# First attention: transposing the attended rows next to the input rows, with one copy for both and the affinity product at the front of the step

## The chip, the core and the metric

The kernel runs on one core of one Trainium2 chip. The metric is device time in microseconds (us) of one execution, as a median of several. A profile is one further execution with the hardware profiler on; its times are counted from the first instruction. The engines are PE (matrix products; its weight loads are listed as PEld), DVE (vector), ACT (scalar), POOL (GpSimd) and SP (which issues DMAs). Each works through its own queue in order, and they wait for each other at semaphores.

## What is computed

Two blocks of attention with a mixture of experts behind each. The change lies in the first attention and in the product that its router needs:

```python
x = x + _L0_xattn_ref(_layernorm(x), ctx_1024, Wq, bq, Wkv, bkv)
x = x + _L0_ffn_ref(_layernorm(x), centroids, ...)       # aff = layernorm(x) @ centroids.T ; one of 8 experts by argmax
x = x + _L1_xattn_ref(_layernorm(x), ctx_1024, ...)
x = x + _L1_ffn_ref(x, ...)                              # two of 8 experts
```

There are 32 sequences of 100 queries and 361 context rows, with 256 features; the first attention has 16 heads of 16 features. The affinities `aff` are, for each sequence, a product of 100 normalised attended rows (256 features) with 256 x 8 centroids.

## The kernel before

The program runs four stages one after the other: attention 0, routing and expert tiles, attention 1, routing and gated tiles. Both attentions come from one function, `attention` (L125), with `layer` 0 or 1. It goes through the sequences in steps (`run_steps`, L79): the steps -1 to 3 and 28 to 32 are written out, and the 24 between them run as a loop of two steps per round. Each engine has its own `step`, and the order of the calls in it is the order of its queue. In a step, three sequences are in work: the step's own, b, gets its scores, exponentials and values; the next one gets its queries, keys, values and row maxima; the one before, `prev`, gets its residual, its normalisation and its affinities.

The order on PE in a step of attention 0 (L530) is: transposes of the next sequence's normalised input rows `xh` (L404) into PSUM bank M0; the second half of its keys (`project_k`, L369 into M1); `max_columns` (L447), which transposes the row maxima of b; the query products (L414); a third of the values (L369); `scores(b, 0)` (L464, L471); row 0 (L439); and from there on the rows 1 to 7, with scores, values (L481) and projections between them. A "row" is the two score products of `score_rows` (L431) for one pair of heads of the next sequence, into bank SM. DVE takes the maxima out of SM (L989). There is one SM buffer, so row j waits until DVE has read row j - 1. Between row 4 and `values(b, 1)` stand the transposes of the attended rows `xp` of `prev` into M1 (`out_transposes`, L498). Between row 5 and `values(b, 2)` stands their product with the centroids, two accumulated products of 8 columns (`out_product`, L512, out of `oT`, which is the tile `avs`). After row 6 comes the first half of the keys of the sequence after next (`start_k`), which waits for `cl`, the low part of the context that POOL makes (L837).

ACT copies the transposed input rows out of M0 (`front`, L656, tile `xT`), makes `ch` (L618), copies keys (`copy_k`, L599), copies the row maxima (`max_columns`, L694, tile `mxT`), and then the queries `qf` (L664). Later in the step, behind the third exponential, it copies the transposed attended rows out of M1 (`copy_out`, L685).

POOL masks the row maxima (`masked_max`, L858, tile `MXM`), for which `scores(b, 0)` waits, and behind that it adds the attention's output to the rows of X (`attended`, L791). DVE masks the queries (`masked_queries`, L980, tile `QM`), for which row 0 waits. Between maxima 5 and 6 it copies the affinities out of M1 (`take_product`, L1048).

Instructions of attention 0 and 1 carry the same names, with a leading `a_`; buffer numbers are left out.

Of the kernel before, what the change touches and what calls it, by code (L numbers as in the profile page):

```python
# [20 lines left out]
ACT = mybir.ActivationFunctionType  # L21
# [7 lines left out]
DC = D // 128  # L29
# [40 lines left out]
def fixed(b):  # L70
    return Batch(b // 2, b % 2, b)
# [53 lines left out]
def attention(nc, layer, t, env):  # L125
# [29 lines left out]
    with ExitStack() as ctx:  # L155
# [22 lines left out]
        xh = sb("xh", [LQ, D])  # L178
        xT = sb("xT", [128, DC, LQ])


# [16 lines left out]
        avs = sb("avs", [128, NG, LQ])  # L198
        oT = avs
        rs = sb("rs", [LQ, H])  # L200
# [163 lines left out]
        def _(pe):  # L364
# [32 lines left out]
            def front(b):  # L397
                pe.wait_ge(xh_ready, b.count(1, 1))
                if b.low == 1:
                    pe.wait_ge(v_evac, 2)  # L400
                    if layer == 1:
                        pe.wait_ge(qtok_ready, 1)
                for c in range(DC):
                    last = nc.tensor.transpose(M0[:, c * LQ:(c + 1) * LQ], xh[:, c * 128:(c + 1) * 128],  # L404
                                               ident[0:LQ, 0:LQ])
                last.then_inc(xT_ps, 1)
                pe.wait_ge(k_evac, b.count(2, 1))
                project_k(b, 1)

            def project(b):  # L410
# [111 lines left out]
            def start_k(nxt, nxt2, prev, tail):  # L522
                pe.wait_ge(v_evac, nxt.count(2, 1))
                if tail:
                    pe.wait_ge(wo_used, prev.count(1, 1))
                first_k(nxt2)
# [3 lines left out]
            def step(b, fr, ahead, back, tail):  # L530
                nxt, nxt2, prev = b.plus(1), b.plus(2), b.plus(-1)

                def rows_of(*pairs):
                    if fr:
                        for j in pairs:
                            score_rows(nxt, j)

                if fr:
                    front(nxt)
                if back:  # L540
                    max_columns(b)
                if fr:
                    project(nxt)
                if back:
                    scores(b, 0)
# [14 lines left out]
                rows_of(*((4,), (2,))[layer])  # L560
                if tail:
                    if fr:
                        pe.wait_ge(v_evac, nxt.count(2, 1))
                    out_transposes(prev, layer == 1, prev.low >= LAG)
                if back:
                    values(b, 1)
                rows_of(*((5,), ())[layer])
                if tail:
                    out_product(prev, layer == 1, prev.low >= LAG)
# [15 lines left out]
            pe.wait_ge(pads_set, 4)  # L585
            run_steps(pe, step)
            if layer == 1:
                for b in (NB, NB + 1):
                    pe.wait_ge(wo_used, b)
                    out_transposes(fixed(b), False, True)  # L590
                    out_product(fixed(b), False, True)

        @block.scalar
        def _(act):
# [58 lines left out]
            def front(b):  # L653
                act.wait_ge(v_ps, b.count(2))
                act.wait_ge(xT_ps, b.count(1, 1))
                nc.scalar.activation(xT[:], M0[:, 0:DC * LQ].rearrange("p (c q) -> p c q", c=DC), ACT.Copy  # L656
                                     ).then_inc(xT_sb, 1)

            def projected(b):
# [37 lines left out]
            def step(b, fr, ahead, back, tail):  # L697
                if fr:
                    front(b.plus(1))
                if ahead:  # L700
                    high_context(b.plus(2))
# [8 lines left out]
                for s in range(NS):  # L710
# [7 lines left out]
                    if tail and layer == 0 and s == 1:  # L718
                        attended_rows(b.plus(-1))
                    if tail and s == 2:  # L720
                        prev = b.plus(-1)
                        copy_out(prev, 0, RC + DC if prev.low >= LAG else DC)
# [21 lines left out]
            input_rows(fixed(0))  # L744
            run_steps(act, step)
            if layer == 1:
                copy_out(fixed(NB), DC, 2 * DC)
                kept(fixed(NB - 1))
                copy_out(fixed(NB + 1), DC, 2 * DC)
# [186 lines left out]
        def _(dve):  # L936
# [106 lines left out]
            def take_product(b, out, routed):  # L1043
                dve.wait_ge(wo_ps, b.count(1, 1))
                if out:
                    last = V_.tensor_tensor(o2[:], M1[0:LQ, 0:D], bob[:], ALU.add)
                if routed:
                    last = V_.tensor_copy(  # L1048
                        env["aff"][:, bass.ds(b.plus(-LAG).at, 1), :].rearrange("q o e -> q (o e)"),
                        M1[0:LQ, AFF:AFF + E])  # L1050
                last.then_inc(wo_used, 1)
# [18 lines left out]
            def step0(b, fr, ahead, back, tail):  # L1070
                nxt, nxt2, prev = b.plus(1), b.plus(2), b.plus(-1)
                if fr:
                    masked_queries(nxt)
                for j in range(NP):
                    if tail and j == 6:
                        take_product(prev, False, True)
                    if fr:
# [47 lines left out]
            input_stats(fixed(0))  # L1125
            run_dve(dve, step, link, dve_own, OWN_PER_ROUND[layer])
            if layer == 1:
# [900 lines left out]
```

## Time and profile before

| | us |
|---|---|
| median of 3 executions (lowest to highest) | 1751.89 (1747.49 to 1752.88) |
| the profiled execution, its own time | 1762.67 |
| its span, from the first to the last instruction | 1760.9 |
| PE busy in the span | 1523.3 (87%) |
| DVE / ACT / POOL busy | 991.2 / 802.1 / 829.9 |

The page of the profile gives the shares of the whole program. The first attention fills the stretch up to about 550 us. For a change in it, the views to read are the ones that go by time: the busy times of stretches, and the timelines of single engines through two steps that follow each other. In a timeline each line has the start and the length in us; a bracket gives the idle time of the engine ahead of the line and what ended it. Lines of like instructions are merged; the length is then from the first one's start to the last one's end.

### The profile page before, as it was taken

What the parts mean: (1) busy time and instruction counts of PE and PEld (TensorE: products, weight loads), DVE (VectorE), ACT (ScalarE), POOL (GpSimd) and SP (SyncE); (2) the same over time, 40 slices, a digit from 0 to 9 for tenths busy, and PEclk for the clock granted to TensorE, in tenths of its full rate; (3) what the DMA queues carried; (4) which work ended last, traced back from release to release, by engine and by line L of the source; (5) the groups of instructions that cost most, each with busy time, mean ns of one, the idle gap of its engine ahead of it and who ended that gap; (6) DMA issues with size and microseconds to landing.
All of it is one profiled execution on the core that took longest, in us unless ns stands there. A gap on an engine that the chain in (4) does not pass through costs nothing. (4 is left out here: it accounts for less than half of the span.)

```text
span 1760.9 us, 48368 instructions
## 1 busy us (share of the span) xinstructions
PE 1523.3 (87%) x16402; PEld 1144.4 (65%) x16403; DVE 991.2 (56%) x2212; ACT 802.1 (46%) x1568; POOL 829.9 (47%) x1145
## 2 busy tenths in 40 slices
PE   5999999999993599999589999999999329999867
PEld 4777777777772367676478888888887214444356
DVE  3666666666663322222247777777777466766544
ACT  3677777777762122222256666666665101111111
POOL 3666666666661111111247666666675103333163
PEclk9999999999995799999799999999999559999989
DMA  5111212011103211111212222221110322333275
GB/s 130 57 58 45 80 56 73 28 32 32 32 9 147 98 33 33 33 33 33 79 34 72 74 86 67 94 68 40 46 47 18 119 97 95 108 109 109 91 210 155
DMA packets 60327, 125.94 MB, mean 72 GB/s; under 512 B 11522, under 2 KB 33286, under 8 KB 56806
## 3 DMA queue, kind: packets, MB, share of 16 engines
q1 hardware_dynamic: 49942, 97.01, 16.6%
q0 software_dynamic: 10320, 28.07, 5.8%
q8 instruction: 41, 0.67, 0.2%
q14 instruction: 24, 0.20, 0.0%
HBM read 92.74 MB, written 32.29 MB: 71 GB/s over the span
## 5 line engine op out<-in xcount | busy, mean ns | idle before, releaser
L989 DVE TENSOR_REDUCE a_mx<-a_SM 100x2 bf16<-100x722 f32 x384 | 351.5, 915 | 214.6 <-PE a_SM L439 209.7
L714 ACT ACTIVATE a_Pr<-a_ST 120x1600 f32<-120x1600 f32 (+3 forms) x192 | 225.2, 1173 | 133.0 <-PE a_ST L471 132.4
L1757 PE MATMUL g_PH<-w,g_xT 128*128 x456 | 207.7, 599 | 0.0
L763 POOL TENSOR_TENSOR a_rstd<-a_ve,a_powers 100x1 f32<-100x1 f32 x192 | 119.2, 621 | 161.4 <-DVE a_ve L959 161.4
L439 PE MATMUL a_SM<-a_KT,a_QM 32*100 32x362 f32 x768 | 155.2, 400 | 43.9 <-DVE a_mx L989 40.1
L481 PE MATMUL a_M<-a_Pr,a_V 120*32 120x100 f32 (+3 forms) x4608 | 174.9, 255 | 0.0
L481 PEld LDWEIGHTS a_M<-a_Pr,a_V 120*32 120x32 f32 (+3 forms) x4608 | 134.7, 119 | 21.3 <-issue 12.5
L1757 PEld LDWEIGHTS g_PH<-w,g_xT 128*128 128x128 f32 x456 | 83.4, 193 | 83.9 <-issue 83.9
L837 POOL TENSOR_TENSOR a_cl<-a_ct,a_ch 128x724 fp32r<-128x724 f32 x64 | 111.5, 1742 | 45.5 <-DVE a_o L1031 43.4
L439 PEld LDWEIGHTS a_SM<-a_KT,a_QM 32*100 32x100 f32 x768 | 62.5, 159 | 101.5 <-DVE a_mx L989 75.8
L369 PE MATMUL a_M<-a_ch,a_wkh 128*128 128x362 f32 x256 | 99.4, 388 | 28.3 <-POOL a_cl L837 28.3
L369 PE MATMUL a_M<-a_wvh,a_ch 128*120 128x256 f32 (+1 forms) x384 | 120.1, 313 | 0.0
L826 POOL TENSOR_TENSOR a_KL<-a_KF,a_KT 128x724 fp32r<-128x724 f32 x64 | 110.9, 1733 | 19.2 <-ACT a_KT L607 19.2
L1807 ACT ACTIVATE g_sg<-g_ab 128x512 f32<-128x512 f32 x57 | 35.9, 630 | 182.0 <-DVE g_ab L1834 182.0
L1495 PE MATMUL e_PH<-w,e_xT 128*128 x256 | 116.7, 599 | 1.1 <-DVE e_xT L1571 1.1
L1515 PE MATMUL e_PY<-w,e_hT 128*128 x512 | 115.9, 379 | 1.5 <-DVE e_hT L1583 1.5
L1463 POOL COPY e_gidx<-toks 128x1 int32 (+1 forms) x32 | 5.9, 183 | 217.3 <-PE e_PX L1484 182.3
L369 PE MATMUL a_M<-a_wvh,a_cl 128*120 128x256 f32 (+1 forms) x384 | 108.2, 282 | 0.0
L369 PE MATMUL a_M<-a_wvl,a_ch 128*120 128x256 f32 (+1 forms) x384 | 108.2, 282 | 0.0
L1515 PEld LDWEIGHTS e_PY<-w,e_hT 128*128 128x128 f32 x512 | 94.9, 190 | 13.8 <-issue 2.2
L471 PE MATMUL a_ST<-a_QM,a_KT 32*120 32x100 f32 (+3 forms) x1536 | 103.0, 304 | 0.0
L599 ACT ACTIVATE a_KF<-a_M,a_bk 128x362 f32<-128x362 f32 x128 | 71.8, 561 | 50.2 <-PE a_M L369 50.0
(203 smaller groups left out, 3559.7 us busy)
## 6 DMA issues: line engine op xcount, KB each, us to landing
w<-in_E_w SPq DMA_DIRECT2D x24, 1024.0 KB, 6.8
a_ct<-in_ctx SPq DMA_DIRECT2D x64, 362.0 KB, 3.0
gated_rows<-g_hs SPq DMA_DIRECT2D x57, 256.0 KB
keep_rows<-a_keep SPq DMA_DIRECT2D x64, 100.0 KB
tile_rows<-e_y SPq DMA_DIRECT2D x32, 128.0 KB, 1.7
b_rows<-in_E_b SPq DMA_DIRECT2D x1, 4096.0 KB
x_rows<-X SPq DMA_DIRECT2D x32, 100.0 KB
X<-x_rows SPq DMA_DIRECT2D x1, 3200.0 KB
```

What stands on the lines that cost most here:

```text
L369: last = nc.tensor.matmul(out, lhs(c), rhs(c), start=(k == 0), stop=(k == len(steps) - 1))
L439: last = nc.tensor.matmul(SM[0:LQ, half, 0:LKP], QM[b.p][rows, chunk, m, :], KT[b.p][rows, chunk, :], start=True, stop=True)
L471: last = nc.tensor.matmul(ST[0:n, r, t * LQ:(t + HT) * LQ], K[rows, chunk, k0:k0 + n], Q[rows, chunk, :, :], start=False, stop=(k == 2 and ...
L481: last = nc.tensor.matmul(M0[VW * j:VW * (j + 1), g * LQ:(g + 1) * LQ], V[b.p][0:n, kt, h, :], Pr[0:n, kt, POS[h] * LQ:(POS[h] + 1) * LQ], ...
L714: nc.scalar.activation(Pr[0:n, s, :].rearrange("p (r q) -> p r q", r=GROUPS), ST[0:n, :, 0:PER * LQ], ACT.Exp, scale=SCALE).then_inc(exp_d ...
L763: nc.gpsimd.tensor_tensor(rstd[k][:], ve[k][:].to_broadcast([LQ, n]), powers[:, 0:n], ALU.pow).then_inc(rstd_ready[k], 1)
L826: nc.gpsimd.tensor_tensor(KL[b.p][:], KF[:], KT[b.p][:], ALU.subtract).then_inc(kl_ready, 1)
L837: nc.gpsimd.tensor_tensor(cl[b.p][:], ct[b.p][:], ch[b.p][:], ALU.subtract).then_inc(cl_ready, 1)
L989: V_.tensor_reduce(pair, SM[0:LQ, :, 0:LK], AX_X, ALU.max).then_inc(max_done, 1)
L1495: last = nc.tensor.matmul(PH[:, h, :], xT[:, c, :], rhs, start=(c == 0), stop=(c == DC - 1))
L1515: last = nc.tensor.matmul(PY[:, 0:D], hT[:, g, :], rhs, start=(g == 0), stop=(g == G - 1))
L1757: last = nc.tensor.matmul(PH[:, p, h, :], xT[p][:, c, :], rhs, start=(c == 0), stop=(c == DC - 1))
```

## The change

Only attention 0 changes. On PE, the transposes of the attended rows leave their place behind row 4. They are made a step later, at the front, right behind those of the input rows and beside them in M0 (`attended_columns`). ACT copies both with one instruction of 400 columns into one tile, `xoT`, of which `xT` and `oT` are now the two halves; the copy behind the third exponential is gone. The product with the centroids (`affinities`) leaves its place behind row 5. It stands at the step's front, between the second half of the keys and `max_columns`, and goes to a free part of the scores' bank ST instead of M1. It waits for the copy, and `scores(b, 0)` now also waits until DVE has taken the affinities. DVE takes them at the front of its step, ahead of `masked_queries`. The first keys of the sequence after next no longer wait for that. Behind the last step, the attended rows of the last sequence are transposed, copied and multiplied by themselves.

```diff
-        xT = sb("xT", [128, DC, LQ])
+        xoT = sb("xoT", [128, (2 - layer) * DC, LQ])
+        xT = xoT[:, 0:DC, :]
...
-        oT = avs
+        oT = avs if layer else xoT[:, DC:2 * DC, :]
...
                 last.then_inc(xT_ps, 1)
+                if layer == 0 and b.low >= 3:
+                    attended_columns(b.plus(-3))
                 pe.wait_ge(k_evac, b.count(2, 1))
                 project_k(b, 1)
+
+            def attended_columns(b):
+                pe.wait_ge(xp_ready, b.count(1, 1))
+                for c in range(DC):
+                    last = nc.tensor.transpose(M0[:, (DC + c) * LQ:(DC + c + 1) * LQ], xp[:, c * 128:(c + 1) * 128],
+                                               ident[0:LQ, 0:LQ])
+                last.then_inc(oT_ps, 1)
+
+            def affinities(b):
...
+                if b.low < NB - 3:
+                    pe.wait_ge(xT_sb, b.plus(3).count(1, 1))
+                else:
+                    pe.wait_ge(oT_sb, b.low - (NB - 4))
+                for c in range(DC):
+                    last = nc.tensor.matmul(ST[0:LQ, GROUPS - 1, 0:E], oT[:, c, :], rows[:, c, :],
+                                            start=(c == 0), stop=(c == DC - 1))
+                last.then_inc(wo_ps, 1)
...
+                late = layer == 0 and tail and b.plus(-2).low >= 0
                 if fr:
                     front(nxt)
+                elif late:
+                    attended_columns(b.plus(-2))
+                if late:
+                    affinities(b.plus(-2))
                 if back:
                     max_columns(b)
                 if fr:
                     project(nxt)
+                if late and back:
+                    pe.wait_ge(wo_used, b.plus(-2).count(1, 1))
                 if back:
                     scores(b, 0)
...
-                if tail:
+                if tail and layer == 1:
...
                     out_transposes(prev, layer == 1, prev.low >= LAG)
...
-                if tail:
+                if tail and layer == 1:
                     out_product(prev, layer == 1, prev.low >= LAG)
...
-                nc.scalar.activation(xT[:], M0[:, 0:DC * LQ].rearrange("p (c q) -> p c q", c=DC), ACT.Copy
+                n = DC
+                if layer == 0 and b.low >= 3:
+                    act.wait_ge(oT_ps, b.plus(-3).count(1, 1))
+                    n = 2 * DC
+                nc.scalar.activation(xoT[:, 0:n, :], M0[:, 0:n * LQ].rearrange("p (c q) -> p c q", c=n), ACT.Copy
                                      ).then_inc(xT_sb, 1)
...
-                    if tail and s == 2:
+                    if tail and layer == 1 and s == 2:
                         prev = b.plus(-1)
                         copy_out(prev, 0, RC + DC if prev.low >= LAG else DC)
...
+                if tail and b.plus(-2).low >= 0:
+                    take_product(b.plus(-2), False, True)
                 if fr:
                     masked_queries(nxt)
                 for j in range(NP):
-                    if tail and j == 6:
-                        take_product(prev, False, True)
                     if fr:
                         maxima(nxt, j)
```

Two places show the new order. The first is PE's queue in the middle of a step of the loop, from row 4 to the first keys of the sequence after next. Before, with the transposes of `xp` (L498) and the product with the centroids (tile `rows`, L512):

```order
L439 MATMUL a_SM<-a_KT,a_QM 100x362 x2
L498 MATMUL a_M<-a_ident,a_xp 128x100 x2
L481 MATMUL a_M<-a_Pr,a_V 32x100 x16
L436 REGISTER_ALU
L439 MATMUL a_SM<-a_KT,a_QM 100x362 x2
L512 MATMUL a_M<-a_rows,a_avs 100x8 x2
L477 REGISTER_ALU
L481 MATMUL a_M<-a_Pr,a_V 32x100 x16
L436 REGISTER_ALU
L439 MATMUL a_SM<-a_KT,a_QM 100x362 x2
L394 REGISTER_ALU
L369 MATMUL a_M<-a_ch,a_wkh 128x362
```

And after, where the rows are L461 and the values L503:

```order
L461 MATMUL a_SM<-a_KT,a_QM 100x362 x2
L503 MATMUL a_M<-a_Pr,a_V 32x100 x16
L458 REGISTER_ALU
L461 MATMUL a_SM<-a_KT,a_QM 100x362 x2
L499 REGISTER_ALU
L503 MATMUL a_M<-a_Pr,a_V 32x100 x16
L458 REGISTER_ALU
L461 MATMUL a_SM<-a_KT,a_QM 100x362 x2
L394 REGISTER_ALU
L369 MATMUL a_M<-a_ch,a_wkh 128x362
```

Between two rows there stand now only the 16 products of values.

The second place is PE's queue at the front of a step, from the transposes of the input rows to the query products (`wq`). Before:

```order
L404 MATMUL a_M<-a_ident,a_xh 128x100 x2
L369 MATMUL a_M<-a_ch,a_wkh 128x362
L369 MATMUL a_M<-a_cl,a_wkh 128x362
L369 MATMUL a_M<-a_ch,a_wkl 128x362
L369 MATMUL a_M<-a_ch,a_wkh 128x362
L369 MATMUL a_M<-a_cl,a_wkh 128x362
L369 MATMUL a_M<-a_ch,a_wkl 128x362
L447 MATMUL a_ST<-a_neg_ident,a_mxr 128x100 x2
L414 MATMUL a_M<-a_xT,a_wq 128x100 x4
```

And after:

```order
L404 MATMUL a_M<-a_ident,a_xh 128x100 x2
L416 MATMUL a_M<-a_ident,a_xp 128x100 x2
L369 MATMUL a_M<-a_ch,a_wkh 128x362
L369 MATMUL a_M<-a_cl,a_wkh 128x362
L369 MATMUL a_M<-a_ch,a_wkl 128x362
L369 MATMUL a_M<-a_ch,a_wkh 128x362
L369 MATMUL a_M<-a_cl,a_wkh 128x362
L369 MATMUL a_M<-a_ch,a_wkl 128x362
L428 MATMUL a_ST<-a_rows,a_xoT 100x8 x2
L469 MATMUL a_ST<-a_neg_ident,a_mxr 128x100 x2
L436 MATMUL a_M<-a_xoT,a_wq 128x100 x4
```

Two transposes and two products now stand ahead of the query products, and the products stand ahead of the row maxima's transposes too.

## Rows read from the trace of the kernel before

**Rows 1.** Busy times of a stretch of the loop: engines, granted clock, DMA share.

```profile
core 0: us, PE busy (x) PEld busy (x) DVE busy (x) ACT busy (x) POOL busy (x), PEclk, DMA share, GB/s
300.00:400.00 100.00, 94.43 (x1570) 76.11 (x1568) 65.31 (x124) 71.37 (x125) 66.68 (x90) 1.00 0.13 39
```

**Rows 2.** Timeline of PE, the front of a long step up to row 0.

```profile
337.16 0.34 PE L404 MATMUL a_M<-a_ident,a_xh 100*128 100x100 f32 x2
337.28 0.41 PE L369 MATMUL a_M<-a_ch,a_wkh 128*128 128x362 f32 x1
...
338.37 0.27 PE L447 MATMUL a_ST<-a_neg_ident,a_mxr 100*128 100x100 bf16 x2
338.47 1.10 PE L414 MATMUL a_M<-a_xT,a_wq 128*128 128x100 f32 x8
...
340.34 0.39 PE L464 MATMUL a_ST<-a_MXM,a_ones_bf 32*121 32x400 bf16 x4
...
341.65 0.41 PE L439 MATMUL a_SM<-a_KT,a_QM 32*100 32x362 f32 x2 [0.31 <-DVE a_QM L980]
```

**Rows 3.** Timeline of PE, the rows 3 to 6 of that step and its end.

```profile
346.44 0.41 PE L439 MATMUL a_SM<-a_KT,a_QM 32*100 32x362 f32 x2 [0.19 <-DVE a_mx L989]
...
347.86 0.40 PE L439 MATMUL a_SM<-a_KT,a_QM 32*100 32x362 f32 x2 [0.23 <-DVE a_mx L989]
...
349.34 0.41 PE L439 MATMUL a_SM<-a_KT,a_QM 32*100 32x362 f32 x2
349.68 0.52 PE L512 MATMUL a_M<-a_rows,a_avs 128*100 128x8 f32 x4
350.12 0.89 PE L481 MATMUL a_M<-a_Pr,a_V 120*32 120x100 f32 x32
350.95 0.40 PE L439 MATMUL a_SM<-a_KT,a_QM 32*100 32x362 f32 x2
351.28 0.43 PE L369 MATMUL a_M<-a_ch,a_wkh 128*128 128x362 f32 x1
...
353.32 0.34 PE L404 MATMUL a_M<-a_ident,a_xh 100*128 100x100 f32 x2
```

**Rows 4.** Timeline of PE, the short step that follows: first scores, row 0, end.

```profile
356.65 0.39 PE L464 MATMUL a_ST<-a_MXM,a_ones_bf 32*121 32x400 bf16 x4 [0.21 <-POOL a_MXM L858]
...
357.49 0.33 PE L439 MATMUL a_SM<-a_KT,a_QM 32*100 32x362 f32 x2
...
369.07 0.34 PE L404 MATMUL a_M<-a_ident,a_xh 100*128 100x100 f32 x2
```

**Rows 5.** Timeline of DVE: masked queries of both steps, one copy of affinities.

```profile
340.32 1.09 DVE L980 TENSOR_TENSOR a_QM<-a_qf,a_mask 128x400 fp32r<-128x400 f32 x1 [1.59 <-ACT a_qf L664]
...
350.62 0.16 DVE L1048 COPY affs<-a_M 100x8 f32 x1
...
356.46 0.58 DVE L980 TENSOR_TENSOR a_QM<-a_qf,a_mask 128x400 fp32r<-128x400 f32 x1 [1.57 <-ACT a_qf L664]
```

**Rows 6.** Timeline of POOL: masked maxima, residual add, low context; then the short step's add.

```profile
339.43 0.85 POOL L858 TENSOR_TENSOR a_MXM<-a_mxT,a_mask_bf 128x400 bf16<-128x400 bf16 x1 [2.43 <-ACT a_mxT L694]
340.24 0.73 POOL L791 TENSOR_TENSOR X<-X,a_o 100x256 f32 x1
...
349.36 1.73 POOL L837 TENSOR_TENSOR a_cl<-a_ct,a_ch 128x724 fp32r<-128x724 f32 x1
...
356.48 1.16 POOL L791 TENSOR_TENSOR X<-X,a_o 100x256 f32 x1
```

**Rows 7.** Timeline of ACT: a copy of 400 columns, then the long step's front.

```profile
334.95 0.50 ACT L730 ACTIVATE a_avs<-a_M 128x400 f32<-128x400 f32 x1 [0.78 <-PE a_M L481]
...
337.60 0.34 ACT L656 ACTIVATE a_xT<-a_M 128x200 f32<-128x200 f32 x1 [0.58 <-PE a_M L404]
...
338.56 0.56 ACT L599 ACTIVATE a_KF<-a_M,a_bk 128x362 f32<-128x362 f32 x1
339.02 0.33 ACT L694 ACTIVATE a_mxT<-a_ST 128x200 bf16<-128x200 f32 x1
```

**Rows 8.** All masked queries of the loop: durations in ns, least, median, greatest.

```profile
L980 DVE TENSOR_TENSOR a_QM<-a_qf,a_mask x24: 574/832/1093, 101.1 to 467.9; 128x400 fp32r<-128x400 f32 x24
```

More of the change, by code:

```diff
@@ L406, in front @@
                 last.then_inc(xT_ps, 1)
+                if layer == 0 and b.low >= 3:
+                    attended_columns(b.plus(-3))
                 pe.wait_ge(k_evac, b.count(2, 1))
                 project_k(b, 1)
+            def attended_columns(b):
[5 more added lines that the diff above has]
+            def affinities(b):
+                if b.low == 0:
+                    pe.wait_ge(rest_loaded, REST_LOADED)
+                if b.low < NB - 3:
[6 more added lines that the diff above has]
+                last.then_inc(wo_ps, 1)
             def project(b):
@@ L567, in step @@
                 rows_of(*((5,), ())[layer])
-                if tail:
+                if tail and layer == 1:
                     out_product(prev, layer == 1, prev.low >= LAG)
@@ L586, in _ @@
             run_steps(pe, step)
+            if layer == 0:
+                attended_columns(fixed(NB - 1))
+                affinities(fixed(NB - 1))
             if layer == 1:
@@ L655, in front, with attended_columns @@
                 act.wait_ge(xT_ps, b.count(1, 1))
-                nc.scalar.activation(xT[:], M0[:, 0:DC * LQ].rearrange("p (c q) -> p c q", c=DC), ACT.Copy
+                n = DC
[3 more added lines that the diff above has]
+                nc.scalar.activation(xoT[:, 0:n, :], M0[:, 0:n * LQ].rearrange("p (c q) -> p c q", c=n), ACT.Copy
                                      ).then_inc(xT_sb, 1)
+            def attended_columns(b):
+                act.wait_ge(oT_ps, b.count(1, 1))
+                nc.scalar.activation(oT[:], M0[:, DC * LQ:2 * DC * LQ].rearrange("p (c q) -> p c q", c=DC), ACT.Copy
+                                     ).then_inc(oT_sb, 1)
             def projected(b):
@@ L699, in step @@
                     front(b.plus(1))
+                elif tail and layer == 0:
+                    attended_columns(b.plus(-2))
                 if ahead:
@@ L745, in _ @@
             run_steps(act, step)
+            if layer == 0:
+                attended_columns(fixed(NB - 1))
             if layer == 1:
@@ L1047, in take_product @@
                 if routed:
+                    src = M1[0:LQ, AFF:AFF + E] if layer else ST[0:LQ, GROUPS - 1, 0:E]
                     last = V_.tensor_copy(
-                        env["aff"][:, bass.ds(b.plus(-LAG).at, 1), :].rearrange("q o e -> q (o e)"),
-                        M1[0:LQ, AFF:AFF + E])
+                        env["aff"][:, bass.ds(b.plus(-LAG).at, 1), :].rearrange("q o e -> q (o e)"), src)
                 last.then_inc(wo_used, 1)
@@ L1126, in _ @@
             run_dve(dve, step, link, dve_own, OWN_PER_ROUND[layer])
+            if layer == 0:
+                take_product(fixed(NB - 1), False, True)
             if layer == 1:
```

## The prediction

> **What bounds the kernel now.** I read first the busy times of a stretch in the loop, to see which engine fills a step, and then the timelines of PE, DVE, POOL and ACT through two steps that follow each other. PE is busy 94.43 of 100 us there at the full granted clock, and no other engine comes near it, while the DMAs have a share of 0.13 [rows 1]. So a step lasts as long as PE's queue with the waits inside it. Two steps of unlike length alternate: the long one runs from 337.16 to 353.32, 16.16 us, the short one from 353.32 to 369.07, 15.75 us [rows 2 to 4].
>
> The difference arises before row 0, and it is the first thing for the reader to see. From its front a long step reaches row 0 after 341.65 - 337.16 = 4.49 us, a short step after 357.49 - 353.32 = 4.17 us [rows 2 to 4]. In the long step PE waits for DVE's masked queries, which took 1.09 us there and 0.58 us in the short one [rows 2, 5]. What sets that length is who begins first, DVE with the masked queries or POOL with its residual add. In the long step POOL begins at 340.24 and DVE at 340.32: POOL needs 0.73 and DVE 1.09. In the short step DVE begins at 356.46 and POOL at 356.48: DVE needs 0.58 and POOL 1.16 [rows 5, 6]. The later one loses about half a microsecond. Over the loop the 24 lengths run from 574 to 1093 ns with their median halfway, so about half of the steps are of each kind [rows 8]. The race is decided by 0.02 to 0.08 us.
>
> The second thing is the middle of a step. The rows there follow DVE: from row 3 to row 4 it is 347.86 - 346.44 = 1.42 us, and PE waits for the maxima at both [rows 3]. From row 4 to 5, where the transposes of the attended rows stand, it is 1.48; from 5 to 6, with the affinity product, 1.61, and at neither does PE wait [rows 3].
>
> **What the change takes away in the middle.** Without the transposes and the product, what is late next is DVE's maximum: neither gap can fall under 1.42. The gain is 0.06 + 0.19 = 0.25 us a step, though more of PE's work than that leaves; the rest turns into waiting. Behind row 6 stands the next obstacle. The first keys begin at 351.28, and they need the low context that POOL finishes at 349.36 + 1.73 = 351.09 [rows 3, 6]. That is a slack of 0.19, out of which the way of the signal must be paid too, and POOL's work has no reason to come earlier relative to row 0. So in a long step at least 0.06 of the 0.25 is given back, and all of it if the signal takes 0.19. I take 0.13 kept as the mean, with 0 and 0.25 as bounds.
>
> **What the change adds at the front.** The two transposes: the pair that stands there takes 337.28 - 337.16 = 0.12 until the next product starts [rows 2]; half of the four passes of the affinity product would be 0.22 [rows 3]. I take 0.18. The product: as it stands in the middle its four passes take 350.12 - 349.68 = 0.44 [rows 3]; four passes like those of the transposes would be 0.24. It is the same instruction as before, without a change of tile shape on both sides, so I take 0.36. PE's work ahead of the query products thus grows by 0.54, with 0.36 and 0.66 as ends. Of cover there is none on PE: row 7, the transposes and the keys follow each other without a gap.
>
> The wider copy on ACT: 0.50 for 400 columns against 0.34 for 200, so 0.16 [rows 7]. ACT's next instructions follow at once, and the copy itself starts 0.18 later, behind the added transposes; the keys' copy and the copy of the row maxima come 0.34 later, at 338.90 and 339.36. The transposes of the row maxima end at 338.37 + 0.27 + 0.54 = 339.18 and don't delay that [rows 2, 7]. So POOL's masked maxima move by 0.34, and its residual add from 340.24 to 340.58 [rows 6]. The copy that is gone behind the third exponential frees ACT where it waits for PE anyway, which I cost at nothing.
>
> Does the product wait for the copy? The copy ends at 337.60 + 0.18 + 0.50 = 338.28; the product's turn comes at 338.37 + 0.18 = 338.55. It does not, with 0.27 to spare. DVE's copy of the affinities, 0.16, now stands ahead of the masked queries, in an idle time of 1.59 [rows 5], and PE's new wait for it ahead of the first scores is long met.
>
> **What this does to row 0.** The masked queries wait for the query products, so DVE could begin them 0.54 later, at 340.32 + 0.54 = 340.86. POOL begins its add at 340.58, 0.28 ahead. In the short step the two shifts turn DVE's lead of 0.02 into a lag of 0.18. **From now on DVE loses the race in every step**, whichever end of the front's price holds for the product: with 0.36 in all it still lags.
>
> When POOL is first, the masked queries end 340.32 + 1.09 - 340.24 = 1.17 after POOL's start, and row 0 starts 341.65 - 341.41 = 0.24 later [rows 2, 5, 6]. In the long step that gives 340.58 + 1.17 + 0.24 = 341.99, 0.34 later than now. In the short step POOL starts at 356.48 + 0.34 = 356.82, and row 0 at 358.23, 0.74 later than now. PE alone would be there earlier: from the first scores to row 0 it needs 357.49 - 356.65 = 0.84 [rows 4], so 340.34 + 0.54 + 0.84 = 341.72 in the long step. The mean of 0.34 and 0.74 is 0.54.
>
> A rule of the Trainium skill bears on this. Its page "SBUF — State Buffer", section "Who interferes with whom", says that a DVE instruction with two inputs in SBUF and a GpSimd instruction that reads SBUF contend for a shared port, that the first to start keeps it for its whole length, and that the other is fully blocked (its summary says to schedule around it by what is off the critical path; here POOL's add is off it, and now goes first). The trace agrees about who waits, but not that all of the loser's length comes behind the winner: the blocked masked queries ended 1.17 after POOL's start, where 0.73 + 0.58 would be 1.31 [rows 5, 6]. By the rule the masked queries would end 0.14 later in each step, 29 x 0.14 = 4 us more; I go by the rows.
>
> **The sum.** A step gains 0.54 at its front and loses 0.13 in its middle: +0.41. Steps with a front and a late product are numbers 2 to 30, 29 of them, 24 in the loop; the written-out ones I take to be like the loop's mean. 29 x 0.41 = 11.9 us. Step 1 loses its pieces in the middle without getting any at the front, about -0.2. The last two steps keep the same chain of rows, transposes, copy and product, part of it ahead of waits; I take 0, within one product and one copy, 0.44 + 0.50 = 0.9 us. In all +11.7. Against the profiled execution's own time that is 1762.67 + 11.7 = 1774; that execution is 0.6% over the median, and the steps' sum carries over unscaled, so on the median it is 1751.9 + 11.7 = 1763.6. With the pair of transposes at 0.12 or 0.22 and the middle's gain at 0.25 or 0, a step comes to between +0.23 and +0.58: 1758.4 to 1768.5.
>
> **Rivals.** *DVE is not blocked more often than now.* For it speaks that the race is decided by hundredths and that both starts move. Then PE sets row 0: 341.72 in the long step, +0.07; in the short step 353.32 + (340.34 - 337.16) + 0.54 + 0.84 = 357.88, +0.39. The mean 0.23 less 0.13 is 0.10, times 29: 1754.6 with step 1, and with the whole 0.25 kept 1751.1. Against it speaks that the add depends on the keys' copy and the row maxima alone, which the product in front of the query products does not push.
>
> *Faster: the front's additions hide.* If the product's weight loads run under the keys, so that only the transposes count (0.18), and the wider copy does not push ACT, then the first scores follow POOL's masked maxima, 0.18 later than in the short step now: row 0 at 356.65 + 0.18 + 0.84 - 353.32 = 4.35 after the front, against a mean of 4.33 now. The middle's 0.25 is then gained almost whole, 0.23 x 29 = 6.7: 1745.0. It decides from where the product costs under about 0.1 instead of 0.36. Against it: the product's 0.44 in the middle, and a copy that is longer by 0.16 in a row of ACT's instructions without a gap.
>
> *Slower still: the product waits for the copy.* If the copy came more than 0.27 later than worked out, the product would hold up the row maxima and the query products behind it in PE's queue, and each 0.1 of it costs 2.9 us; with 0.2 more it is 1769. No row suggests it.
>
> **How the numbers follow.** Chances: the forecast 0.66, slower still 0.07, not blocked 0.20, faster 0.07. The likeliest gives 1763.6. The range goes from 1752 (into the second case, whose ends are 1751.1 and 1754.6) to 1770, which leaves out the faster case and the tails, some 0.15. A measurement of this kernel can tell about 0.3%, or 5.3 us, from no change: under 1746.6 is faster, over 1757.1 slower. The forecast lies over it with all but a little of its own range; the not-blocked case lies inside; the faster one reaches over its bound with about all of its chance. So slower 0.70, same 0.22, faster 0.08.
>
> **What would show it.** Right: all masked queries of the loop near or over 0.9 us; steps of one length, some 16.3 to 16.4 us; row 0 waiting for DVE in each; rows 4, 5 and 6 at 1.42 with waits for the maxima; the first keys waiting for the low context now and then. Wrong: masked queries of 0.58 in half of the steps or more, row 0 less than 4.6 us behind the front, or the product's four passes taking under 0.2 between the keys and the row maxima.

## The result: 0.4% slower, about half of what was predicted

The changed kernel takes 1757.5 us (median of 5 runs, 1756.2 to 1758.9) against 1751.9 us for the kernel before (median of 5, 1747.5 to 1752.9). The ratio is 1.0038, 95% interval 1.0025 to 1.0051, so the change costs between 4.4 and 8.9 us. The prediction was 1763.6 us, or +11.7. The direction and the mechanism hold; the size is too large, about twice the 5.6 us between the medians and half as much again as the 7.8 us that the traces show below. The interval holds both.

The two traces are compared by stretches, not by their spans: the profiled execution of before is the longer one, 1760.9 us against 1755.1, because its last stage, with the gated experts, took 308.8 us there and 292.4 here, counted from its first matrix product. The change doesn't touch that stage, and in the traces of the nine experiments it took 291.6 to 293.6. The first steps, up to the front of step 2, took 66.59 and 69.49; over all kernels run here this varied from 66.4 to 69.7 without following any edit.

What the change moves lies in the first attention's steps. From the front of step 2 to the front of step 30 there are 445.60 us in the trace of before and 453.44 in that of after: +7.84. In the 24 steps of the loop the mean length goes from 15.96 to 16.20, 24 x 0.24 = 5.8; the four written-out steps among them (2, 3, 28, 29) go from 15.65 to 16.15, 4 x 0.50 = 2.0. The short and long steps of before are gone: the loop of after has only steps of 16.2 us, as one sees in the fronts of the step below, 361.01 and 377.21.

The first view is the busy times of the same stretch as in [rows 1]: PE is busy 92.19 of 100 us where it was 94.43. The engine that bounds the kernel does its work as before, but waits more.

```profile
core 0: us, PE busy (x) PEld busy (x) DVE busy (x) ACT busy (x) POOL busy (x), PEclk, DMA share, GB/s
300.00:400.00 100.00, 92.19 (x1530) 75.17 (x1526) 65.92 (x123) 70.78 (x119) 61.57 (x85) 1.00 0.13 39
```

The second is the timeline of PE through one step of after. It answers to [rows 2 to 4].

```profile
361.01 0.34 PE L404 MATMUL a_M<-a_ident,a_xh 100*128 100x100 f32 x2
361.18 0.33 PE L416 MATMUL a_M<-a_ident,a_xp 100*128 100x100 f32 x2
361.30 0.41 PE L369 MATMUL a_M<-a_ch,a_wkh 128*128 128x362 f32 x1
...
362.37 0.44 PE L428 MATMUL a_ST<-a_rows,a_xoT 128*100 128x8 f32 x4
362.67 0.25 PE L469 MATMUL a_ST<-a_neg_ident,a_mxr 100*128 100x100 bf16 x2
362.75 1.10 PE L436 MATMUL a_M<-a_xoT,a_wq 128*128 128x100 f32 x8
...
364.64 0.39 PE L486 MATMUL a_ST<-a_MXM,a_ones_bf 32*121 32x400 bf16 x4
...
365.81 0.41 PE L461 MATMUL a_SM<-a_KT,a_QM 32*100 32x362 f32 x2 [0.16 <-issue]
...
372.01 0.41 PE L461 MATMUL a_SM<-a_KT,a_QM 32*100 32x362 f32 x2 [0.23 <-DVE a_mx L1034]
...
373.44 0.41 PE L461 MATMUL a_SM<-a_KT,a_QM 32*100 32x362 f32 x2 [0.19 <-DVE a_mx L1034]
...
374.86 0.41 PE L461 MATMUL a_SM<-a_KT,a_QM 32*100 32x362 f32 x2 [0.19 <-DVE a_mx L1034]
375.20 0.43 PE L369 MATMUL a_M<-a_ch,a_wkh 128*128 128x362 f32 x1
375.47 0.33 PE L369 MATMUL a_M<-a_cl,a_wkh 128*128 128x362 f32 x1
...
377.21 0.34 PE L404 MATMUL a_M<-a_ident,a_xh 100*128 100x100 f32 x2
```

Three things are to be seen. The transposes push the keys by 361.30 - 361.01 - 0.12 = 0.17, and the product takes 362.67 - 362.37 = 0.30 until the next matmul starts. Row 0 stands 365.81 - 361.01 = 4.80 behind the front, where it stood 4.49 and 4.17. The bracket of row 0 names "issue" here and DVE's masked queries in every second step; but in all 24 steps of the loop row 0 starts 0.24 us after the masked queries end, as it did in the long steps of before. And rows 4, 5 and 6 are now 373.44 - 372.01 = 1.43 and 1.42 apart, with a wait for DVE's maxima at each, where rows 5 and 6 of [rows 3] waited for nothing.

Then POOL and DVE in that step, which answer to [rows 5, 6], and ACT, which answers to [rows 7]:

```profile
363.59 0.85 POOL L903 TENSOR_TENSOR a_MXM<-a_mxT,a_mask_bf 128x400 bf16<-128x400 bf16 x1 [2.50 <-ACT a_mxT L735]
364.40 0.73 POOL L836 TENSOR_TENSOR X<-X,a_o 100x256 f32 x1
...
373.36 1.74 POOL L882 TENSOR_TENSOR a_cl<-a_ct,a_ch 128x724 fp32r<-128x724 f32 x1
```

```profile
362.95 0.17 DVE L1094 COPY affs<-a_ST 100x8 f32 x1 [0.38 <-PE a_ST L428]
364.60 0.97 DVE L1025 TENSOR_TENSOR a_QM<-a_qf,a_mask 128x400 fp32r<-128x400 f32 x1 [1.47 <-ACT a_qf L705]
```

```profile
361.55 0.50 ACT L692 ACTIVATE a_xoT<-a_M 128x400 f32<-128x400 f32 x1 [0.69 <-PE a_M L416]
361.95 0.80 ACT L650 ACTIVATE a_ch<-a_ct 128x724 fp32r<-128x724 f32 x1
...
363.10 0.34 ACT L735 ACTIVATE a_mxT<-a_ST 128x200 bf16<-128x200 f32 x1
```

POOL's residual add starts at 364.40, DVE's masked queries at 364.60: POOL is first, by 0.20, and the masked queries take 0.97. The group of all masked queries of the loop (the answer to [rows 8]; least, median and greatest duration in ns) says that this is so in every step:

```profile
L1025 DVE TENSOR_TENSOR a_QM<-a_qf,a_mask x24: 965/970/972, 105.4 to 478.0; 128x400 fp32r<-128x400 f32 x24
```

### The profile page after: what moved, and what is told of

Its sections match the earlier page's. It is cut to its first block and busy times, and to the rows that moved or that the text cites. A ratio compares the mean times of both kernels' runs of the same rounds, so it can differ in the third digit from the quotient of the medians.

```text
span 1755.1 us, 48307 instructions
## 1 busy us (share of the span) xinstructions
PE 1520.9 (87%) x16402; PEld 1145.0 (65%) x16403; DVE 1002.7 (57%) x2212; ACT 800.5 (46%) x1539; POOL 821.2 (47%) x1145
## 5 line engine op out<-in xcount | busy, mean ns | idle before, releaser
L461 PE MATMUL a_SM<-a_KT,a_QM 32*100 32x362 f32 x768 | 156.9, 405 | 57.2 <-DVE a_mx L1034 51.4
L503 PE MATMUL a_M<-a_Pr,a_V 120*32 120x100 f32 (+3 forms) x4608 | 175.5, 256 | 0.2 <-ACT a_Pr L757 0.2
L503 PEld LDWEIGHTS a_M<-a_Pr,a_V 120*32 120x32 f32 (+3 forms) x4608 | 135.2, 120 | 28.1 <-issue 23.2
L461 PEld LDWEIGHTS a_SM<-a_KT,a_QM 32*100 32x100 f32 x768 | 62.7, 159 | 121.9 <-DVE a_mx L1034 96.0
```

Of the source, the lines that this page charges most:

```text
L461: last = nc.tensor.matmul(SM[0:LQ, half, 0:LKP], QM[b.p][rows, chunk, m, :], KT[b.p][rows, chunk, :], start=True, stop=True)
L503: last = nc.tensor.matmul(M0[VW * j:VW * (j + 1), g * LQ:(g + 1) * LQ], V[b.p][0:n, kt, h, :], Pr[0:n, kt, POS[h] * LQ:(POS[h] + 1) * LQ], ...
```

## The experiments

The theory: a step pays at its front for work that stood in its middle, and above all DVE's masked queries now lose to POOL's residual add in all steps instead of half. The main rivals: what is added at the front costs its length on PE whoever is first, or the attended rows' work was free where it stood. All comparisons below are with runs of the kernel before beside them, with medians of 1749.8 to 1751.5 us. Besides the time I give the mean length of the 24 loop steps and the mean distance of row 0 from the front: before 15.96 and 4.33, after 16.20 and 4.81; differences of them are taken ahead of rounding. These two come from one traced execution of each kernel; who wins the race in its other executions is not known.

**Without the work.** In `none` the transposes, the copies and the products of the attended rows are left out of the first attention. The affinities are filled once from input rows, so the routing behind it differs, and the lengths of the steps say more here than the whole time.

```diff
-                if layer == 0 and b.low >= 3:
-                    attended_columns(b.plus(-3))
...
-                late = layer == 0 and tail and b.plus(-2).low >= 0
+                late = False
...
```

> The kernel after without the transposes, copies and products of the attended rows in the first attention; the affinities are filled once from input rows instead, so the routing and the output differ. It gives the price of these pieces in their old place (before less this) and in their new place (after less this). My theory: in the middle they cost about 0.22 us a step, so before is some 6 us over this kernel; at the front about 0.47 us a step, so after is some 13 us over it. The masked queries alternate between 0.58 and 1.09 us as in the kernel before. Rival (the pieces cost what PE spends on them, whatever place): before and after are both about 0.8 us a step, 22 us, over this kernel.

Measured: 1744.6 us, ratio 0.997 (0.9958 to 0.9981); steps of 15.69, row 0 at 4.32. Without this work a step is 0.27 shorter than before and 0.51 shorter than after. So the work costs 0.27 in the middle and 0.51 at the front, and a price that doesn't depend on the place falls. In `none` masked queries of 0.58 and 1.09 alternate again, as in [rows 5]:

```profile
244.93 1.09 DVE L1012 TENSOR_TENSOR a_QM<-a_qf,a_mask 128x400 fp32r<-128x400 f32 x1 [1.59 <-ACT a_qf L696]
...
260.79 0.58 DVE L1012 TENSOR_TENSOR a_QM<-a_qf,a_mask 128x400 fp32r<-128x400 f32 x1 [1.56 <-ACT a_qf L696]
```

**The race taken out of after.** In `a_add_waits` POOL's residual add waits until the masked queries are done; nothing else changes. What needs the add's result, DVE's statistics of the attended rows, starts in after at 367.08, 1.95 us behind the add's end; the wait moves the add by about 1.1 us.

```diff
                 if tail and layer == 0:
+                    if fr:
+                        pool.wait_ge(qm_ready, nxt.count(1, 1))
                     attended(prev)
```

> The kernel after, with POOL's residual add made to wait for the masked queries of the same step, so that DVE has always begun first. My theory (the masked queries behind POOL's add cost row 0 some 0.3 us in every step): masked queries 0.58 us, row 0 at about 4.5 us behind the front instead of 4.80, steps of 15.9 us instead of 16.2, some 9 us less than after and a little under before. Rival (PE's added work at the front is the whole cost, the wait for DVE only fills time that PE needs anyway): steps within 0.05 us of after.

Measured: 1746.0 us, ratio to before 0.9974 (0.9964 to 0.9984); steps of 15.81, row 0 at 4.45. The wait takes 0.39 us off each loop step of after, and 453.44 - 442.66 = 10.8 us off the way from step 2 to step 30. The timelines of DVE, POOL and PE in one step whose front is at 241.36:

```profile
244.96 0.58 DVE L1027 TENSOR_TENSOR a_QM<-a_qf,a_mask 128x400 fp32r<-128x400 f32 x1 [1.48 <-ACT a_qf L705]
245.78 0.41 PE L461 MATMUL a_SM<-a_KT,a_QM 32*100 32x362 f32 x2
245.83 0.73 POOL L836 TENSOR_TENSOR X<-X,a_o 100x256 f32 x1 [1.03 <-DVE a_QM L1027]
```

The masked queries start no earlier than in after, 244.96 - 241.36 = 3.60, but need 0.58; row 0 waits for nobody. That the front's length on PE alone made the loss is refuted: its work is all still there.

**The race taken out of before.** `b_add_waits` puts the same two lines into the kernel before.

> The kernel before with the same wait of POOL's add for the masked queries. My theory: the long steps of 16.15 us become like the short ones of 15.75, 12 of them in the loop, 0.4 x 12 = 5 us less than before. Rival: no difference, or the add and what follows it on POOL come later and cost as much.

Measured: 1742.0 us, ratio 0.9954 (0.9941 to 0.9967); steps of 15.70, row 0 at 4.09. All 27 masked queries in the loop and the three steps behind it are short, as the group shows:

```profile
L982 DVE TENSOR_TENSOR a_QM<-a_qf,a_mask x27: 574/576/577, 100.9 to 508.8; 128x400 fp32r<-128x400 f32 x27
```

The gain was larger than I expected, since a long step doesn't only become like a short one: its first scores come at 3.16 to 3.18, the short one's at 3.33, and it now takes mostly 15.62 to 15.66 where the other takes 15.74.

The two kernels with the wait give the account of the change. Without the race it costs 15.81 - 15.70 = 0.11 a step: row 0 comes 0.35 later, at 4.45 instead of 4.09, and the middle is shorter by 0.24. The race costs before 15.96 - 15.70 = 0.26 and after 16.20 - 15.81 = 0.39. The change's 0.24 are thus 0.11 for moved work and 0.13 for the race that DVE now always loses.

**Each part alone.** `transposes_alone` has the transposes and the wide copy at the front, the product behind row 5 as before.

```diff
...
-                if late:
-                    affinities(b.plus(-2))
...
                 rows_of(*((5,), ())[layer])
+                if late:
...
+                    affinities(b.plus(-2))
...
```

> Half of the change: the transposes and the wide copy at the front, the affinity product back behind row 5 in bank M1. My theory: PE's front grows by 0.17 us only, the masked queries start at 3.32 us and POOL's add at 3.40 because of the wide copy, so DVE wins; row 0 at 4.40, the gap from row 4 to 5 falls to 1.42 and that from 5 to 6 stays 1.61; steps of 15.9 us, within 2 us of before. Rival (PE's work ahead of row 0 sets its time): row 0 at 4.33 + 0.17 = 4.50, steps of 16.05, 3 us over before.

Measured: 1747.1 us, ratio 0.9987 (0.9975 to 0.9999); steps of 15.88, row 0 at 4.37. The wide copy delays POOL (its add starts at 3.40 instead of 3.08 and 3.15), the masked queries less (3.31 and 3.33): DVE is first in every step, though in the loop by less than 0.1. One step, front at 225.78, on DVE, POOL and PE:

```profile
229.08 0.58 DVE L1030 TENSOR_TENSOR a_QM<-a_qf,a_mask 128x400 fp32r<-128x400 f32 x1 [1.73 <-ACT a_qf L710]
229.18 1.08 POOL L841 TENSOR_TENSOR X<-X,a_o 100x256 f32 x1
229.35 0.39 PE L486 MATMUL a_ST<-a_MXM,a_ones_bf 32*121 32x400 bf16 x4 [0.29 <-POOL a_MXM L908]
```

Against `b_add_waits`, where DVE is also always first, row 0 comes 0.28 later. This cost goes by way of ACT and POOL: the copy starts later, behind the added transposes, and is longer, and the first scores wait for POOL's masked maxima in every step, 0.19 to 0.29 us. In `b_add_waits` they wait for them, 0.21 to 0.23, only in every second step.

`product_alone` leaves the transposes and a copy of their own behind row 4, and has only the product at the front, ahead of the row maxima.

```diff
-                if layer == 0 and b.low >= 3:
-                    attended_columns(b.plus(-3))
...
-                if tail and layer == 1:
+                if tail:
                     if fr:
                         pe.wait_ge(v_evac, nxt.count(2, 1))
                     out_transposes(prev, layer == 1, prev.low >= LAG)
...
```

> The other half: the transposes and their copy behind row 4 as before, the affinity product a step later at the front, ahead of the row maxima. My theory: the masked queries start 0.3 us later, at 3.45 us, while POOL's add stays at 3.1 (no wide copy), so DVE loses in every step; row 0 at 3.12 + 1.17 + 0.24 = 4.53, the gap from 5 to 6 falls to 1.42; steps of 15.95 us, as the mean before, with masked queries near 0.85 us in all of them. Rival (the race isn't what decides): masked queries of 0.58 us in half of the steps.

Measured: 1749.9 us, ratio 1.000 (0.9989 to 1.001); steps of 15.97, row 0 at 4.52. Here DVE is the one that is delayed, and POOL is first in every step; DVE's and POOL's timelines of two steps in a row, fronts at 244.46 and 260.39:

```profile
247.54 0.73 POOL L821 TENSOR_TENSOR X<-X,a_o 100x256 f32 x1
247.89 0.81 DVE L1010 TENSOR_TENSOR a_QM<-a_qf,a_mask 128x400 fp32r<-128x400 f32 x1 [1.48 <-ACT a_qf L694]
...
263.54 0.73 POOL L821 TENSOR_TENSOR X<-X,a_o 100x256 f32 x1
263.80 0.91 DVE L1010 TENSOR_TENSOR a_QM<-a_qf,a_mask 128x400 fp32r<-128x400 f32 x1 [1.47 <-ACT a_qf L694]
```

The parts don't add up. Alone they change a step by -0.08 and +0.02, together by +0.24. The transposes alone let DVE win always, the product alone makes it lose always, and both together make it lose.

**The product behind the query products.** `product_behind_queries` is after with the product moved behind the query products, so that it no longer delays them.

```diff
                 last.then_inc(q_ps, 1)
+                if between is not None:
+                    affinities(between)
                 pe.wait_ge(k_evac, b.count(2, 2))
...
```

> The kernel after with the affinity product put behind the query products instead of ahead of the row maxima; PE has the same work in the same stretch ahead of row 0. My theory: the masked queries start 0.3 us earlier, about 3.33 us behind the front, and POOL's add stays at 3.40, so DVE wins the race by some 0.07 us; row 0 at about 4.5, steps of 15.9 us, some 9 us less than after. Rival (PE's work ahead of row 0 sets it): the same as after.

Measured: 1745.1 us, ratio 0.9971 (0.9959 to 0.9982); steps of 15.76, row 0 at 4.45. A step is 0.44 us shorter than in after, by the order of eight query passes and four product passes alone. Row 0 comes where it came in `a_add_waits`, which took the race out in another way. DVE leads by 0.08:

```profile
245.00 0.58 DVE L1027 TENSOR_TENSOR a_QM<-a_qf,a_mask 128x400 fp32r<-128x400 f32 x1 [0.17 <-ACT a_qf L707]
245.08 1.09 POOL L838 TENSOR_TENSOR X<-X,a_o 100x256 f32 x1
```

**Two copies instead of one.** `two_copies` starts from this kernel and copies the attended columns by themselves, behind the copy of the row maxima; POOL then starts sooner.

```diff
-                    last = nc.tensor.transpose(M0[:, (DC + c) * LQ:(DC + c + 1) * LQ], xp[:, c * 128:(c + 1) * 128],
+                    last = nc.tensor.transpose(ST[:, 2, c * LQ:(c + 1) * LQ], xp[:, c * 128:(c + 1) * 128],
...
                     max_columns(b)
+                if fr and layer == 0 and tail and b.plus(-2).low >= 0:
+                    attended_columns(b.plus(-2))
...
```

> product_behind_queries with two copies instead of one: the input rows by themselves at the front, the attended rows (in a free bank of ST) behind the copy of the row maxima. ACT's way to the row maxima becomes shorter by 0.16 us. My theory: that brings POOL's add to 3.24 us, ahead of the masked queries at 3.33, so DVE loses again: masked queries near 1 us, row 0 at 4.65, steps of 16.0 us, some 6 us over product_behind_queries. Rival (the wide copy's length costs time): row 0 earlier by up to 0.16, steps of 15.6 to 15.7.

Measured: 1756.7 us, ratio 1.0031 (1.0016 to 1.0046); steps of 16.10, row 0 at 4.74. POOL is first again, as expected, and the masked queries take 0.91 and 0.98. But the experiment doesn't show the race alone. The second copy also delays the copy of the queries, and PE's product with the centroids waits for the second copy: the first scores come at 3.88 to 3.90 instead of 3.57 to 3.65, and with the 0.84 from them to row 0 that gives 4.73 by itself. The loss of 0.34 a step has two causes here that reach row 0 at about the same time; how much is left with one of them gone was not tried.

**A better kernel.** `spread` goes back to the middle. POOL waits as in `b_add_waits`, the transposed rows get a tile of their own, and the product comes a step later in two halves, behind the value products ahead of row 3 and behind the scores ahead of row 4.

```diff
+                if late:
+                    product_half(b.plus(-2), 0)
                 rows_of(*((3,), ())[layer])
                 if back:
                     scores(b, 2)
+                if late:
+                    product_half(b.plus(-2), 1)
...
+                    if late:
+                        pe.wait_ge(wo_used, b.plus(-2).count(1, 1))
                     out_transposes(prev, layer == 1, prev.low >= LAG)
...
```

> From the kernel before, with POOL's add waiting for the masked queries: the transposes stay behind row 4, and the two halves of the product go one step later behind values(b, 0) and scores(b, 2), that is into the gaps from row 2 to 3 and from 3 to 4, where PE waits 0.2 us for the maxima. My theory: the gap from row 5 to 6 falls from 1.61 to 1.42 at no cost elsewhere, unless the first keys wait for POOL's low context: steps of 15.5 to 15.6 us instead of 15.65 and 15.74, 3 to 5 us less than b_add_waits. Rival: the halves lengthen their gaps, or the keys wait; no gain.

Measured: 1740.7 us, ratio 0.9947 (0.9933 to 0.9961); steps of 15.69, no shorter on average than the 15.70 of `b_add_waits`. The hoped-for gain is there at row 6, which follows row 5 by 1.42 instead of 1.61, but it is given back just ahead: row 5 follows row 4 by 1.77 in every second step and by 1.57 in the others, where before it was 1.48. PE's timeline there, and DVE's copy that it waits for:

```profile
264.89 0.41 PE L439 MATMUL a_SM<-a_KT,a_QM 32*100 32x362 f32 x2
265.52 0.39 PE L498 MATMUL a_M<-a_ident,a_xp 100*128 100x100 f32 x2 [0.22 <-DVE affs L1070]
...
266.66 0.41 PE L439 MATMUL a_SM<-a_KT,a_QM 32*100 32x362 f32 x2
```

```profile
265.08 0.17 DVE L1070 COPY affs<-a_M 100x8 f32 x1 [0.24 <-PE a_M L521]
```

The transposes write to the bank that the affinities are read from, so they wait for the copy, and this wait I had put there myself. `spread_early` therefore moves both halves of the product one row earlier, and the copy one maximum:

```diff
                     scores(b, 1)
+                if late:
+                    if fr:
+                        pe.wait_ge(v_evac, nxt.count(2, 1))
+                    product_half(b.plus(-2), 0)
                 rows_of(*((2,), (1,))[layer])
                 if back:
                     free_m0(nxt, fr)
                     values(b, 0)
+                if late:
+                    product_half(b.plus(-2), 1)
                 rows_of(*((3,), ())[layer])
...
```

> The kernel spread once more, with the two halves of the affinity product one row earlier each: the first behind the second scores, ahead of row 2 (with the wait for the V copies that the middle of the step has anyway), the second behind the first value products, ahead of row 3; DVE copies the affinities one maximum earlier. In spread the transposes behind row 4 waited for DVE's copy of the affinities, 0.22 us in one step of two, so that row 4 to row 5 took 1.77 and 1.58. If that wait is the whole cause, the copy now lies one maximum (0.92 us) ahead of the transposes, they wait for nothing, and row 4 to 5 returns to the 1.48 of the kernel before in every step: steps of 15.55 and 15.42 instead of 15.84 and 15.52, mean 15.49, 0.19 less than spread, 24 x 0.19 = 4.6 us, about 1736 us, ratio 0.992. The rival: the time between rows 4 and 5 is PE's own work behind the new places, and moving the product's halves only moves it: row 4 to 5 stays at 1.6 to 1.8, or rows 1 to 3 grow beyond 1.42 by a half product of 0.2, and the time stays within 1 us of spread's 1740.7.

Measured: steps of mostly 15.57 and 15.44, mean 15.52, 0.17 less than `spread`; the wait is gone and row 5 follows row 4 by 1.48 or 1.49:

```profile
249.28 0.41 PE L439 MATMUL a_SM<-a_KT,a_QM 32*100 32x362 f32 x2 [0.23 <-DVE a_mx L1013]
249.62 0.39 PE L498 MATMUL a_M<-a_ident,a_xp 100*128 100x100 f32 x2
250.77 0.41 PE L439 MATMUL a_SM<-a_KT,a_QM 32*100 32x362 f32 x2
```

So the cause of the wait is shown. From step 2 to 30 that trace takes 434.32 us against 438.51, 4.2 less. In the whole time it shows only weakly: the median is 1740.7 (1734.6 to 1741.3), ratio 0.9935 (0.9916 to 0.9954), while the runs of before beside it read 1.7 us higher than those beside `spread`. The intervals of the two overlap. Both beat the kernel before and the changed one; that the second beats the first is seen in the steps and not settled by the times.

## Why the prediction was right in kind and wrong in size

**The race: right.** The step that carried the forecast was that DVE would lose in every step, with POOL's add at 340.58 - 337.16 = 3.42 behind the front. It starts at 3.39 to 3.41, all 24 masked queries of the loop take 965 ns or more, and `a_add_waits` shows that this is worth 0.39 a step. The time alone would not have told: 1757.5 lies nearer to the 1754.6 of the rival "not blocked more often" than to 1763.6. The durations decide against that rival. Of the signs, row 0 waiting for DVE in each step holds by its distance of 0.24 from the masked queries' end; the profile's brackets name DVE in half of the steps only.

**How long the loser takes: right.** The forecast went by the masked queries ending 1.17 after POOL's start. In after they end at 364.60 + 0.97 = 365.57, 1.17 after 364.40; in `product_alone` at 248.70, 1.16 after 247.54, and at 264.71, 1.17 after 263.54. The rule of the Trainium skill ("SBUF — State Buffer", "Who interferes with whom"), by which the second instruction is fully blocked, would put the end 0.73 + 0.58 = 1.31 after POOL's start. No run here shows so late an end: the rule is right on who waits, and by it the end would be 0.14 too late.

**Row 0: 0.47 later, predicted 0.54.** The miss is the short step. There I moved POOL's add by 0.34, from 3.16 to 3.50, as in the long step; it starts at 3.40 in both. So row 0 is at 4.80 or 4.81 in both, where the forecast had 4.83 and 4.91. What I overlooked is slack on ACT. I had ACT's next instructions follow the copy at once; but in before the copy of the keys starts 0.04 after PE's last key product ends, in the long steps as in the short ones. The short step of before on ACT and PE, and the copy of the keys in after:

```profile
353.93 0.80 ACT L618 ACTIVATE a_ch<-a_ct 128x724 fp32r<-128x724 f32 x1
354.71 0.56 ACT L599 ACTIVATE a_KF<-a_M,a_bk 128x362 f32<-128x362 f32 x1
```

```profile
354.35 0.32 PE L369 MATMUL a_M<-a_ch,a_wkl 128*128 128x362 f32 x1
```

```profile
362.65 0.55 ACT L631 ACTIVATE a_KF<-a_M,a_bk 128x362 f32<-128x362 f32 x1
```

From the making of `ch` to the copy of the keys it takes 354.71 - 353.93 = 0.78 there and 0.73 in the long step, but 362.65 - 361.95 = 0.70 in after. So about 0.08 of the 0.34 was free in the short step and 0.03 in the long one; the add moved by 0.24 and 0.32. The product's price, taken at 0.36, was 0.30, and the transposes, 0.18, were 0.17. Since POOL's start sets row 0 in after, the product's size doesn't reach it; that of the transposes does, through the later start of the copy.

**The middle: 0.23 kept, predicted 0.13.** This is the larger of the two mis-sized terms. From row 0 to row 7 a step of before takes 10.81 on average, one of after 10.58. I let the low context take half of the 0.25 back. It takes nothing: in after it ends at 373.36 + 1.74 = 375.10, the keys start at 375.20, right behind row 6, without a wait. Two things were wrong. The slack of 0.19 that I read is that of a long step, and I used it for both kinds; the short step, whose row 0 is at 357.49 [rows 4], has another. Its low context and its keys, from the timelines of POOL and PE of the kernel before:

```profile
364.98 1.74 POOL L837 TENSOR_TENSOR a_cl<-a_ct,a_ch 128x724 fp32r<-128x724 f32 x1
```

```profile
367.06 0.43 PE L369 MATMUL a_M<-a_ch,a_wkh 128*128 128x362 f32 x1
```

The slack is 367.06 - 366.72 = 0.34 there, more than the whole gain. And I saw no reason for POOL to come earlier relative to row 0. In after it starts the low context 373.36 - 365.81 = 7.55 behind row 0; the long step had 349.36 - 341.65 = 7.71 [rows 2, 6], the short one 364.98 - 357.49 = 7.49. Against the long step, most of it is that the last of DVE's statistics of the residual rows, on which POOL waits before this, follows row 0 by 367.89 - 365.81 = 2.08 instead of 343.86 - 341.65 = 2.21. First the long step of before, then after:

```profile
343.86 0.15 DVE L959 TENSOR_SCALAR a_ve<-a_mv 100x1 f32<-100x1 f32 x1
```

```profile
367.89 0.15 DVE L1004 TENSOR_SCALAR a_ve<-a_mv 100x1 f32<-100x1 f32 x1
```

**The sum.** Per loop step +0.47 - 0.23 = +0.24 instead of +0.54 - 0.13 = +0.41. That is 24 x 0.17 = 4.1 us, all that lies between the 11.9 of the forecast and the 7.8 of the trace. That the written-out steps are like the loop's mean was wrong too, but nearly cancels, by luck: all of before's were short, so that four of them lose 0.50 each instead of 0.41, while step 30, counted at 0.41 in the forecast, belongs to a stretch that loses 0.13. From its front to DVE's first instruction of the next stage, which waits for a DMA, it is 46.13 us in before and 46.26 in after, though the last affinities are there 38.21 us behind that front in before and 39.40 in after. Step 1, which I had gain 0.2, gains nothing: 15.87 us in both. The 5.6 us between the medians are 2.2 less than the trace shows for these steps; with the spread of the executions the runs don't settle that rest.

**The rivals.** The wide copy costs what was said, 0.50, and pushes POOL: the faster case, in which the front's additions hide, falls. The product did not wait for the copy (362.05 against 362.37), so neither did the slower one come true. Of my list of signs, steps of 16.3 to 16.4 came out at 16.2, and the keys that were to wait for the low context now and then never did.

## What to carry to other kernels

When two engines begin an operation within one or two tenths of a microsecond and the second is stretched by up to half a microsecond, look first at who wins, and put the order down with a semaphore where the winner is known to matter; in the kernel before this one wait was worth 0.46%, about as much as the whole change under study cost. Price a move by the chain that ends last behind it: the transposes cost little on PE, but the wider copy reached the first scores through ACT and POOL. And where steps alternate, read a slack in each kind, not in one for both.

## What the runs showed of the hardware

The order of two instructions that start 0.2 us apart or less is worth 0.26 us a step in before, where DVE loses in every second step, and 0.39 in after. When DVE is first, POOL's add takes 1.06 to 1.16 instead of 0.73, and what needs its result starts later anyway (in the short step of before the add ends at 356.48 + 1.16 = 357.64, DVE's statistics start at 358.69); when POOL is first, DVE's instruction ends 1.17 after POOL's start, however much later it began itself (0.08 later it took 1.09, 0.20 later 0.97, 0.26 later 0.91, 0.35 later 0.81). That is 0.44 after the add's end, and POOL's masked maxima, which run ahead of the add, do the same to a DVE instruction that starts early enough: in step 2 of `transposes_alone` the masked queries start at 70.27, when the masked maxima run until 69.64 + 0.85 = 70.49; they take 0.65 instead of 0.58 and end 0.43 after them, though they start 0.18 ahead of the add. The four passes of the same product took 0.44 until the next matmul in the middle of the step [rows 3] and 0.30 between the keys and the row maxima; why was not tried.
